# State stage of a selective scan: input and output rows made once and spread by one-pass picks

## What is computed

```python
delta = softplus(x @ Wd + bd)
Bm = x @ WB + bB          # one value per token and state
Cm = x @ WC + bC          # one value per token and state
A = -exp(A_log)
def step(h, (x_t, d_t, B_t, C_t)):
    bar_A = exp(minimum(d_t * A, 2.0))
    bar_B = clip(d_t * B_t, -2.0, 2.0)
    h = clip(bar_A * h + bar_B * x_t, -100.0, 100.0)
    y = sum_over_states(h * C_t) + x_t * D
```

## Time and profile before

| | before |
|---|---|
| median of 3 runs | 3990.86 us |
| the profiled execution | 3990.96 us |
| its span, first to last instruction | 3989.2 us |
| mean granted TensorE clock | 0.932 of full speed |
| TensorE busy over the span | 3506.6 us (88%) |
| VectorE busy over the span | 2973.8 us (75%) |
| ScalarE busy over the span | 2431.2 us (61%) |
| GpSimd busy over the span | 1399.8 us (35%) |
| softplus stage, first TensorE instruction to the next stage's first | 27.6 to 43.0 us |
| state stage, to its last VectorE instruction | 43.0 to 233.8 us |
| first TensorE instruction after the state stage and its check | 234.7 us, then 244.0 us |

### The profile page before, as it was taken

The page is one execution under the profiler, slowest core; times in us unless marked ns, Lnnn a source line. Parts: engine busy times, 40 slices in busy tenths (PEclk is TensorE's granted clock), DMA queues, the critical chain, the costliest instruction groups (busy, mean ns, idle before and its releaser), DMA issues. The chain is left out here.

```text
span 3989.2 us, 103143 instructions
## 1 busy us (share of the span) xinstructions
PE 3506.6 (88%) x41105; PEld 2146.2 (54%) x41105; DVE 2973.8 (75%) x5746; ACT 2431.2 (61%) x4558; POOL 1399.8 (35%) x640
## 2 busy tenths in 40 slices
PE   7979778888859968999999999999999986999898
PEld 3347533333337835666666666666666663222786
DVE  5957757777738967787787787787787764887585
ACT  3336437777728836676667677667677662456573
POOL 3720011111100006675676676666576640000000
PEclk8979869999979979999999999999999997899899
DMA  1000047777602002322322322322322211100000
GB/s 40 0 6 6 14 154 230 233 230 231 205 12 69 12 0 61 97 62 57 95 62 59 94 64 57 96 64 55 97 63 57 61 48 59 35 21 17 12 17 11
DMA packets 174520, 285.74 MB, mean 72 GB/s; under 512 B 36819, under 2 KB 76628, under 8 KB 172116
## 3 DMA queue, kind: packets, MB, share of 16 engines
q1 hardware_dynamic: 173460, 278.40, 23.9%
q10 hardware_dynamic: 576, 0.69, 0.1%
HBM read 103.97 MB, written 74.45 MB: 45 GB/s over the span
## 5 line engine op out<-in xcount | busy, mean ns | idle before, releaser
L2280 POOL TENSOR_TENSOR b2f_norm<-b2f_norm,b2f_minus_half 128x16 f32<-128x16 f32 x192 | 555.1, 2911 | 277.2 <-DVE b2f_norm L2621 277.2
L2270 POOL TENSOR_TENSOR b2f_q<-b2f_q,b2f_q_part 128x1024 f32<-128x1024 f32 x96 | 228.2, 2377 | 642.0 <-DVE b2f_q_part L2611 642.0
L1702 ACT ACTIVATE b1a_weights<-b1a_b_ps 128x512 f32<-128x512 f32 x512 | 277.2, 596 | 40.4 <-PE b1a_b_ps L1627 38.3
L2563 ACT ACTIVATE b2f_v_rows<-b2f_q_ps 128x1024 f32<-128x1024 f32 x96 | 98.3, 1024 | 265.2 <-PE b2f_q_ps L2342 146.4
L1817 DVE TENSOR_REDUCE b1a_tops<-b1a_a_ps 128x1 f32<-128x512 f32 (+3 forms) x512 | 244.6, 502 | 20.3 <-PE b1a_a_ps L1583 18.8
L1534 POOL TENSOR_SCALAR b1a_k_op<-b1a_k_op,b1a_extra 128x1024 bf16<-128x1024 bf16 x32 | 90.7, 2845 | 447.7 <-DMA b1a_k_op<-part_copies 410.4
L1702 ACT ACTIVATE b3a_weights<-b3a_b_ps 128x512 f32<-128x512 f32 (+3 forms) x384 | 161.2, 502 | 136.9 <-PE b3a_b_ps L1637 135.7
L2620 DVE TENSOR_REDUCE b2f_norm<-xn 128x16 f32<-128x1024 f32 x192 | 234.2, 1220 | 13.3 <-ACT xn L2504 6.2
L2513 ACT ACTIVATE b2f_prob<-b2f_odd_ps,b2f_bias,b2f_norm 128x64 f32<-128x64 f32 x768 | 232.7, 447 | 4.7 <-DVE b2f_bias L2637 3.5
L2513 ACT ACTIVATE b2f_prob<-b2f_even_ps,b2f_bias,b2f_norm 128x64 f32<-128x64 f32 x768 | 232.6, 451 | 2.3 <-DVE b2f_bias L2637 2.3
L1710 ACT ACTIVATE b1a_e_sb<-b1a_e_ps 128x512 f32<-128x512 f32 x256 | 153.0, 598 | 122.5 <-PE b1a_e_ps L1569 119.0
(11 more groups left out here) (514 smaller groups left out, 9317.4 us busy)
## 6 DMA issues: line engine op xcount, KB each, us to landing
b2f_values<-b2f_v_rows SPq DMA_DIRECT2D x1534, 64.0 KB, 2.0
position_scratch<-b1a_e_sb SPq DMA_DIRECT2D x128, 512.0 KB, 4.0
b1a_band<-position_scratch SPq DMA_DIRECT2D x128, 384.0 KB
b2f_wqkv<-in_b2f_wqkv SPq DMA_DIRECT2D x6, 1536.0 KB, 7.5
b2f_turn<-in_c_rotary SPq DMA_DIRECT2D x6, 1024.0 KB, 8.4
b1f_raw<-in_b1f_both SPq DMA_DIRECT2D x9, 512.0 KB, 3.7
part_copies<-b1a_parts SPq DMA_DIRECT2D x12, 256.0 KB
b2f_wo<-in_b2f_wo SPq DMA_DIRECT2D x6, 512.0 KB, 9.5
```

The source lines that it names most:

```text
L1702: act.activation(weights[:, s % P_RING, c, lo:QW], b_room(s, c)[:, lo:QW], ACT.Exp).then_inc(S.exps_ready, 1)
L2270: pool.tensor_tensor(G.q[:, g % 2], G.q[:, g % 2], G.q_part[:], ALU.add) \
L2280: pool.tensor_tensor(part, part, G.minus_half[:, 0:HEADS], ALU.pow) \
```

## The change

The rows of all states are now made once, in the softplus stage. A new weight `b0a_wbc` holds `[WB, WC, WB, WC]` side by side (64 of 128 columns used, the rest zero). Four more matmuls (`r_ps`) multiply `xn` by it. VectorE adds the bias and rounds to the one-pass matmul format (`F32R`) into `rows`; on partitions 32 to 63, where the same 32 rows stand once more, it then replaces the rounded value by what the rounding lost (`... - part`). So `rows` holds 32 rounded heads and 32 rounded tails. A 0/1 matrix `pick` (128 x 32, fetched, rounded on GpSimd) selects head and tail of one row: `spread` now multiplies `rows` by one broadcast column of `pick`, in the one-pass format, in place of `xn` by a column of weights.

With the bias already in, `raw` and `hc` become plain products of two tensors (`tensor_tensor`) in place of `scalar_tensor_tensor`. The clip of `raw` and all other steps stay as they are. Two more arrays are fetched on SP inside the layer norm. The untaken step by step version changes in the same way.

```diff
                 def input_product(u):
-                    spread(b_ps, w.wb[:, s:s + 1], b).then_inc(S.b_ready, 1)
+                    spread(b_ps, s, b).then_inc(S.b_ready, 1)
                 def output_product(u):
-                    spread(c_ps, w.wc[:, s:s + 1], b).then_inc(S.c_ready, 1)
+                    spread(c_ps, STATES + s, b).then_inc(S.c_ready, 1)
...
-                def spread(ps, weight, b):
+                def spread(ps, row, b):
                     for j in range(halves):
-                        ins = pe.matmul(ps[:, j], weight.to_broadcast([P, P]),
-                                        xn[:, cols(b * halves + j, QW)], start=True, stop=True)
+                        ins = pe.matmul(ps[:, j], pick[:, row:row + 1].to_broadcast([P, P]),
+                                        rows[:, cols(b * halves + j, QW)], start=True, stop=True)
...
-                    dve.scalar_tensor_tensor(out=raw[:, u % 2], in0=whole(b_ps), scalar=w.bb[:, s:s + 1],
-                                             in1=delta[:, cols(b, T)], op0=ALU.add, op1=ALU.mult) \
+                    dve.tensor_tensor(raw[:, u % 2], whole(b_ps), delta[:, cols(b, T)], ALU.mult) \
                         .then_inc(S.b_read, 1)
...
-                    dve.scalar_tensor_tensor(out=hc[:, u % 2], in0=whole(c_ps), scalar=w.bc[:, s:s + 1],
-                                             in1=h[:, u % 3], op0=ALU.add, op1=ALU.mult) \
+                    dve.tensor_tensor(hc[:, u % 2], whole(c_ps), h[:, u % 3], ALU.mult) \
                         .then_inc(S.hc_ready, 1)
...
# softplus_delta
+            @block.gpsimd
+            def _(pool):
+                pool.tensor_copy(pick_rounded[:], pick[:]).then_inc(S.picked, 1)
+                pool.wait_ge(S.picked, 1)
...
                         .then_inc(S.u_ready, 1)
+                for q in range(QUARTERS):
+                    pe.matmul(r_ps[:, q], w.wbc[:], xn[:, cols(q, QW)], start=True, stop=True) \
+                        .then_inc(S.rows_ready, 1)
...
                                   ALU.add, ALU.max).then_inc(S.stored, 1)
+                for q in range(QUARTERS):
+                    dve.wait_ge(S.rows_ready, q + 1)
+                    dve.tensor_scalar(rows[:, cols(q, QW)], r_ps[:, q], w.bias, None, ALU.add) \
+                        .then_inc(S.headed, 1)
+                    dve.wait_ge(S.headed, q + 1)
+                    part = rows[tails, cols(q, QW)]
+                    dve.scalar_tensor_tensor(out=part, in0=r_ps[tails, q], scalar=w.bias[tails],
+                                             in1=part.bitcast(F32), op0=ALU.add, op1=ALU.subtract) \
+                        .then_inc(S.tailed, 1)
                 dve.wait_ge(S.tail_ready, 1)
                 dve.wait_ge(S.stored, 1)
                 dve.tensor_tensor(delta[:], delta[:], tail[:].rearrange("p q n -> p (q n)"),
                                   ALU.add).then_inc(S.stored, 1)
                 dve.wait_ge(S.stored, 2)
+                dve.wait_ge(S.tailed, QUARTERS)
...
+    "c_pick_states": all_rows(np.tile(np.eye(2 * STATES, dtype=np.float32), (2, 1))),
```

More of the change, by code:

```diff
@@ L597, with ssm_states @@
 SUM_LIMIT = 0.999 * H_LIMIT * H_LIMIT
-def ssm_states(nc, K, w, name, xn, delta, flat, peak, stepwise, fetch=()):
+def ssm_states(nc, K, w, name, xn, delta, rows, pick, flat, peak, stepwise, fetch=()):
     units = [(s, b) for s in range(STATES) for b in range(B)]
@@ L772, in block0_weights @@
     w = Names(wd=first("b0a_wd", [P, P]), small=first("b0a_small", [P, 5 * STATES + 8]),
+              wbc=first("b0a_wbc", [P, P]), pick=first("b0a_pick", [P, 2 * STATES], source="c_pick_states"),
               stock=weight_stock(M, W, later, "b0m", 4),
@@ L785, in block0_attn @@
         wd, small = weights.wd, weights.small
-        w = Names(wb=small[:, 0:16], wc=small[:, 16:32], bb=small[:, 32:48],
-                            bc=small[:, 48:64], a=small[:, 64:80], d=small[:, 80:81],
+        w = Names(bias=small[:, 84:85], wbc=weights.wbc, a=small[:, 64:80], d=small[:, 80:81],
                             bd=small[:, 81:82], ln_w=small[:, 82:83], ln_b=small[:, 83:84])
@@ L792, in block0_attn @@
             delta = Memory(nc, inner).sb("b0a_delta", [P, N])
-            softplus_delta(nc, K, w, wd, xn, delta)
-            ssm_states(nc, K, w, "b0s", xn, delta, flat, peak[:], stepwise=False, fetch=fetch)
+            rows = Memory(nc, inner).sb("b0a_rows", [P, N], F32R)
+            pick = Memory(nc, inner).sb("b0a_pick_rounded", [P, 2 * STATES], F32R)
+            softplus_delta(nc, K, w, wd, xn, delta, rows, weights.pick, pick)
+            ssm_states(nc, K, w, "b0s", xn, delta, rows, pick, flat, peak[:], stepwise=False,
+                       fetch=fetch)
             over = clipped_somewhere(nc, K, peak)
             with nc.If(over > 0):
-                ssm_states(nc, K, w, "b0w", xn, delta, flat, peak[:], stepwise=True)
+                ssm_states(nc, K, w, "b0w", xn, delta, rows, pick, flat, peak[:], stepwise=True)
             with nc.Else():
@@ L816, in block0_attn, with softplus_delta @@
         layer_norm(nc, K, "b0n", flat, x, gain=w.ln_w, offset=w.ln_b, add_to=x)
-def softplus_delta(nc, K, w, wd, xn, delta):
+def softplus_delta(nc, K, w, wd, xn, delta, rows, pick, pick_rounded):
+    tails = slice(2 * STATES, 4 * STATES)
     with ExitStack() as ctx:
@@ L824, in softplus_delta @@
         tail = M.sb("sp_tail", [P, QUARTERS, QW])
-        with stage(nc, "u_ready", "tail_ready", "stored", "act_chain") as (block, S):
+        r_ps = M.ps("sp_rows", [P, QUARTERS, QW])
+        with stage(nc, "u_ready", "tail_ready", "stored", "rows_ready", "headed", "tailed", "picked",
+                   "act_chain") as (block, S):
+            @block.gpsimd
+            def _(pool):
+                pool.tensor_copy(pick_rounded[:], pick[:]).then_inc(S.picked, 1)
+                pool.wait_ge(S.picked, 1)
             @block.tensor
@@ L2873, in layouts @@
          v["L0_attn_A_log"], col(v["L0_attn_D_param"]), col(v["L0_attn_bd"]), col(v["L0_attn_ln_w"]),
-         col(v["L0_attn_ln_b"]), np.zeros((P, 4), np.float32)], axis=1)
+         col(v["L0_attn_ln_b"]),
+         col(all_rows(np.tile(np.concatenate([v["L0_attn_bB"], v["L0_attn_bC"]]), 2))),
+         np.zeros((P, 3), np.float32)], axis=1)
+    a["b0a_wbc"] = np.concatenate([v["L0_attn_WB"], v["L0_attn_WC"]] * 2
+                                  + [np.zeros((P, P - 4 * STATES), np.float32)], axis=1)
     a["b0m_both"] = np.stack([v["L0_attn_up_w"].reshape(4, P, 4, P).transpose(1, 0, 2, 3),
```

## The result

The median of ten runs is 3981.32 us (3974.74 to 3992.18), against 3990.80 us (3986.45 to 3997.51) for ten runs of the kernel before. The ratio is 0.9979, with a 95% interval of 0.9969 to 0.9989. The forecast was 3979.3, with 3976 to 3983 as its own range and 3976 to 3986 with three of the rivals. The profiled execution of the changed kernel took 3985.77 us, its span is 3984.0 us, so this one execution is 4.4 us above its median and only 5.2 us shorter than the profiled one of before.

A forecast was written before the change was run, and what follows sets the result against it. VectorE was taken to bound the state stage, TensorE close behind. Softplus +1.7, start -5.1, units -7.7, end -0.6 gave -11.7 us, from 3990.96 to 3979.3 us, own range 3976 to 3983.

The forecast's parts named there:

- What bounds the stage: State stage: VectorE bounds it, TensorE close behind; 4.1 us over 30 units are waits for TensorE.
- Softplus stage: Four added VectorE pairs cost 5.8 us, 4.1 hidden in a pause; the final add comes 1.7 us late.
- bound of 2.5 for waits: Softplus stage: the loss is 2.5 us if each of eight waits costs 0.1 us more.
- Start: From the state stage's start to the first scan: 5.65 us in place of 10.76, a gain of 5.1.
- Units: Thirty state-stage units: 167.3 us becomes 159.6, a gain of 7.7 from ended TensorE waits and cheaper VectorE products.
- The rule weighed in the prediction: VectorE with a PSUM source: 1.19 us for old and new form alike, so plain products gain nothing.
- End: From the 31st scan to the last pair: 10.3 us taken in place of 10.88, a gain of 0.6.
- (a): State stage: TensorE's clock stays at half, 5.48 us per unit; total 3985.6 us, chance 0.12.
- (b): VectorE's raw and hc: extra time belongs to operands, not form; 3.7 us stay, total 3983.0, chance 0.04.
- (c): State-stage picks cost two records like today's; waits and start stay, total 3988.5 us, chance 0.04.
- (d): State stage: new products hold up GpSimd, each unit grows by 2.3 us; total 4047, chance 0.05.
- (e): Later stages meet the clock in another state and lose some 5 us; total 3984.5, chance 0.05.

The follow-up runs named there:

- Before_tt: The kernel before with only VectorE's raw and hc made plain products, biases of B and C left out; 30 units took 165.51 us, against 167.3 before.
- picks32: The changed kernel with its picks as 32-bit matmuls of two records each; median 3993.67 us, ratio to before 1.0002, 30 units 163.8 us.
- wide version: The changed kernel with rows made by two VectorE operations over 2048 tokens instead of eight over 512; ratio to before 0.9970.
- keep_stt: The changed kernel with raw and hc kept as scalar_tensor_tensor adding a zero; 30 units took 163.16 us, against 159.5 in the changed kernel.
- rows_unused: Softplus stage of the changed kernel makes the rows, but the state stage is that of before and ignores them; 30 units took 165.6 us.
- busy: The changed kernel with TensorE repeating each output product three times before the one that counts; 30 units took 160.2 us, clock 0.99.
- repetition: The changed kernel run once more without any change; median 3983.15 us over ten runs, ratio to before 0.9980, 30 units 159.52 us.

## Right or wrong, step by step

**What bounds the stage.** Right. The reading from 0.15 us between two starts, that TensorE held VectorE up without being booked as idle, carried some 2.5 of the 7.7 us forecast for the units. Before_tt and picks32 show it by making VectorE shorter and leaving TensorE as it was.

**Softplus stage, +1.7 foreseen, +2.25 measured.** The step that was mis-sized is the cost of a pair. I let each bias operation start 0.08 us before the end of the tail operation ahead of it. Measured, all eight start 0.78 us apart (35.79, 36.57, 37.35), 6.24 us in place of 5.8. The final add thus came 2.14 us later counted from the stage's first matmul, and another 0.1 us was lost ahead of the stage. The bound of 2.5 for waits held. One thing that sets these operations apart from hc and raw is where they begin: the tail operation works on partitions 32 to 63, the others on all from 0 on. In the wide version the bias operation, behind the clamp, starts 0.09 us before the clamp's end, but the final add, behind the tail operation, 0.03 us after that one's end, though it does not read the rows. Whether the change of partitions is the cause wasn't tried.

**Start, -5.1 foreseen, -4.65 measured.** Matmuls and products as priced. Of the 0.6 us that clip and GpSimd's product could cost each other 0.46 came about: the clip took 1.16 us, and the scan came at 6.11 in place of 5.65. I had taken the better end, where the steady state's 4.28 us against 2.34 already spoke for the other. By the Trainium skill, page "SBUF — State Buffer", section "Who interferes with whom", an operation of VectorE in a two-port mode and one of GpSimd exclude each other for their whole length. The trace agrees to 0.13 us: the clip ends 0.56 us behind the product, and alone it takes 0.69.

**Units, -7.7 foreseen, -7.80 measured.** Split as foreseen: 4.1 for the waits (keep_stt: 167.31 - 163.16 = 4.15) and 3.7 for the form (163.16 - 159.51 = 3.65). Of the waits, though, the one early wait of 1.7 us goes without the picks (rows_unused); I had put all of them down to TensorE's load, and this one hangs on its clock. The new product takes 1215 and 1224 ns, the row of another block gave 1222. The rule weighed in the prediction, by the Trainium skill, page "VectorE: DVE Perf Modes", section on the TRN2 errata, of equal cost for any form with a PSUM source does not hold here: with the same operands 1276 and 1284 ns with a scalar, 1215 and 1224 without.

**End, -0.6 foreseen, -0.71 measured,** and 10.2 to 11.9 us over all profiles of the changed kernel, which are near the two ends worked out for full and half clock (10.0 and 11.8). That the table shows -0.71 is luck: the 10.3 taken stands for neither, and with the third profile's 11.86 the end is a loss of 1.0. Nor do fewer c records make the gain: with as many as before, at full clock, the end takes 10.2.

**Rivals.** (a) The clock did fall, to 0.86 in the mean of the stage, and came back each time (four y records take 1.88 us at 124.67 and 3.50 at 129.98); the units stayed at 5.32, and busy shows that a full clock gives nothing more. By the rival's own figures, 5.5 and 5.4, a unit at half clock would be 5.45 and not 5.48. (b) fell by keep_stt, apart from the scalar itself. (c) is picks32: its median of 3993.67 us lies 0.7 below that of before on its chip (3994.35), where 2.5 less had been worked out; in its own stretch it is 2.1 less. (d) did not occur: the product takes 4.29 us. (e) was named with 5 us at a chance of 0.05. It stays open: scatter of that size is there in both kernels, but the medians keep less than the lead that the profiles show at the third block's start (next paragraph).

**The total.** The median of the first ten runs is 9.5 us below before, the repetition's 11.2, the two stages' own account 9.3 to 11.0. That they agree so well is in part luck, for two things outside the forecast offset each other. Gains that I had not counted are, in the mean of three profiles each, 1.9 us to the router and 3.4 us in the layer norm after the expert stage. That one took 21.4 us at a granted clock of 0.61 in two profiles of before and 19.0 at 0.73 in the third, 16.9 at 0.90, 17.0 and 17.8 in the changed kernel, and in the variants anything from 16.9 to 21.4: the two profiles of the wide version had 17.9 and 21.4. At the third block's start, counted from the softplus stage's first matmul, the changed kernel is thus 14.5 us ahead in the mean of three profiles each. The medians of the whole keep 9.5 and 11.2 of that, so by these means some 3 to 5 us are lost behind it, which is no more than single profiles scatter by. By what, no run shows.

## What to carry to other kernels

When two engines look equally busy in a loop, compare start to start distances of the leading one within a unit: a wait of 0.15 us that no view books as idle shows there, and two engines that hand work back and forth cost the mean of both chains, so shortening one gave only half here (1.8 of 3.7 us). Moving work into another engine's pause is priced by the pause and by the number of operations: eight of 512 columns cost 6.24 us, two of 2048 cost 4.75. And where a program's single runs scatter by 10 us, a change of 10 us is read from its own stretch. Its 30 units repeat to 0.03 us, but its end, where the clock decides, came out at 10.2 or 11.9 us for one kernel: one profile is not enough there.

## What the hardware showed that was not expected

- One and the same program took 3979.57 to 3999.99 us in ten executions on one chip. In one block it took 1832.7 and 1822.1 us in two sessions, and it reaches the softplus stage's first matmul anywhere from 27.7 to 31.9 us (the changed kernel) or 27.6 to 32.0 (before).
- VectorE's clip of 0.69 us took 1.16 us when GpSimd's product was under way.
- The time from the check to the router's first matmul was 8.7 to 9.2 us without the rows in the softplus stage and 6.2 to 8.0 with them; more code to skip didn't lengthen it.
- TensorE's clock was 0.86 in the mean with pauses of 2.4 us between bursts of some 3 us, or of some 0.7 where a burst ran slow. It fell at times inside a burst that had begun at full clock (at 129.98). With three more picks in each unit and pauses of 1.0 us it was 0.99.
- Four more matmuls in the softplus stage shifted the falls of TensorE's clock in the stage behind it: with the rows made and not used, an early wait of 1.7 us was gone.
